# Inverse roots of the last layer norm for groups of four tiles instead of two, their rows scaled two steps later

## The reference

```
x = _layernorm(x + _L0_gnn_ref(x, ...))                 # attention over the edges into a node
x = _layernorm(x + _L1_gnn_ref(x, edge_attr_64, ...))   # attention with edge features and a gated skip
_layernorm(x): (x - mean) / sqrt(var + 1e-5)            # over the 256 features of a row
```

## Time and profile before

| | |
|---|---|
| time, three runs | 1277.13 us median (1275.6 to 1277.79) |
| the profiled execution | 1276.99 us |
| its span, first to last instruction | 1275.2 us |
| mean granted TensorE clock | 0.978 of full speed |
| busy share of the span | PE 92%, DVE 82%, POOL 67%, ACT 65% |
| the stage Output | from about 1092 us to the end |
| chain that ended last, by engine | PE 59%, DVE 15%, issue 12%, POOL 7%, ACT 3% |

### The profile page before, as it was taken

The page is one execution under the profiler, slowest core; times in us unless marked ns, Lnnn a source line. Parts: engine busy times, 40 slices in busy tenths (PEclk is TensorE's granted clock), DMA queues, the critical chain, the costliest instruction groups (busy, mean ns, idle before and its releaser), DMA issues.

```text
span 1275.2 us, 28369 instructions
## 1 busy us (share of the span) xinstructions
PE 1171.5 (92%) x6982; PEld 1022.2 (80%) x6982; DVE 1044.4 (82%) x3794; ACT 830.0 (65%) x2783; POOL 852.2 (67%) x1074
## 2 busy tenths in 40 slices
PE   2899999999998699999999699999999995799995
PEld 2788999989896478888878599899999994688884
DVE  2667777777778789999999799999999987789895
ACT  0366666666667766666666766656666668589996
POOL 6688888888873355545554567677666753288887
PEclk9899999999999899999999999999999998799998
DMA  7568888888884388778887787777767743355652
GB/s 209 164 223 288 268 271 262 260 272 268 267 265 133 100 273 261 246 252 252 259 249 235 214 241 210 217 220 220 224 201 220 226 144 110 124 184 187 185 192 94
DMA packets 208795, 276.99 MB, mean 217 GB/s; under 512 B 40044, under 2 KB 140419, under 8 KB 208633
## 3 DMA queue, kind: packets, MB, share of 16 engines
q1 hardware_dynamic: 187913, 223.83, 55.8%
q0 software_dynamic: 19264, 50.85, 13.2%
q10 hardware_dynamic: 1456, 0.49, 0.2%
HBM read 159.67 MB, written 117.12 MB: 217 GB/s over the span
## 4 chain that ended last, share of the span: by engine, by line
PE 59%; DVE 15%; issue 12%; POOL 7%; ACT 3%; DMA 2%; another core or an unknown queue 1%; SPq 1%; DVEq 0%; POOLq 0%; ACTq 0%
PE banks L751 20%; PE banks L864 7%; PE banks L741 6%; PE banks L1392 5%; POOL out L1545 4%; PE banks L854 3%; PE banks L1227 3%; POOL output_r L1551 3%; DVE AT L1253 3%; PE banks L866 3%; PE banks L1379 2%; PE banks L1397 2%; PE banks L1220 2%; PE banks L953 2%; PE banks L1377 2%
## 5 line engine op out<-in xcount | busy, mean ns | idle before, releaser
L751 PE MATMUL banks<-m_ext,node_XT 128*128 128x257 f32 x1568 | 376.6, 383 | 0.1
L751 PEld LDWEIGHTS banks<-m_ext,node_XT 128*128 128x128 f32 x1568 | 285.7, 192 | 32.9 <-issue 0.3
L777 DVE SCALAR_TENSOR_TENSOR node_X<-banks,node_be,node_X 128x256 f32<-128x256 f32 x392 | 169.5, 474 | 82.1 <-ACT node_be L703 54.2
L678 POOL TENSOR_TENSOR node_r<-node_vv,half 128x4 f32<-128x4 f32 (+1 forms) x202 | 214.0, 1059 | 17.0 <-POOL node_vv L673 0.2
L709 ACT ACTIVATE node_XT<-banks 128x512 f32<-128x512 f32 x196 | 117.3, 599 | 131.0 <-PE banks L741 122.3
L673 POOL TENSOR_SCALAR node_vv<-node_mv 128x4 f32<-128x4 f32 (+1 forms) x202 | 58.2, 288 | 196.9 <-DVE node_mv L785 177.7
L716 ACT ACTIVATE node_sq<-node_X 128x256 f32<-128x256 f32 x392 | 157.8, 408 | 0.0
L690 ACT ACTIVATE node_X<-node_X,node_r 128x256 f32<-128x256 f32 x326 | 146.0, 496 | 1.4 <-POOL node_r L678 1.4
L770 DVE BATCH_NORM_STATS2 node_st<-node_X 128x6 f32<-128x256 f32 x392 | 145.5, 413 | 1.6 <-issue 1.0
L741 PE MATMUL banks<-ident,node_X 128*128 128x128 f32 x784 | 122.5, 280 | 20.1 <-issue 10.8
L831 POOL DMA_INDIRECT ring<-in_x,src_col x100 | 107.0, 1070 | 26.4 <-issue 14.4
(11 more groups left out here) (265 smaller groups left out, 2731.4 us busy)
## 6 DMA issues: line engine op xcount, KB each, us to landing
node_X<-in_x SPq DMA_DIRECT2D x196, 256.0 KB
out<-node_X SPq DMA_DIRECT2D x196, 256.0 KB
ring<-rows SPq DMA_DIRECT2D x210, 128.0 KB
rows<-ring SPq DMA_DIRECT2D x100, 256.0 KB
rows<-ring SPq DMA_DIRECT2D x200, 128.0 KB
MB<-keeps SPq DMA_DIRECT2D x40, 320.0 KB, 4.6
store<-rows SPq DMA_DIRECT2D x90, 128.0 KB
MB<-picks SPq DMA_DIRECT2D x50, 128.0 KB
```

The lines of the kernel that those rows point to most:

```text
L678: pool.tensor_tensor(r[:, s % 4, NT * lo:NT * hi], v, self.c.half[:, NT * lo:NT * hi], ALU.pow).then_inc(self.roots, 1)
L751: last = pe.matmul(ps[:, NT * o + k, 0:D + 1], self.XT[:, o, k * D + h * P:k * D + (h + 1) * P], c.m_ext[:, h, :], start=(h == 0), stop=(h ...
L777: last = dve.scalar_tensor_tensor(out=X[:, n % U, k, :], in0=ps[:, b + k, 0:D], scalar=self.be[:, n % 4, k:k + 1], in1=X[:, n % U, k, :], ...
```

## The change

The groups become two single tiles, 23 groups of four (tiles 2 to 93) and three pairs (tiles 94 to 99). Rows of a group of more than two are scaled from step last+9 on instead of last+7. So every row n of a group of four is scaled in step n+12 (row k has n = last-3+k, and its step is last+9+k) and scattered in step n+13. The pairs at the end keep last+7, but the running maximum holds them back: row 93 is scaled in step 105, and rows 94 to 97 then in step 105 too, 98 in step 106 and 99 in step 107. Scatters 93 to 97 all stand in step 106. The pow and the epsilon stay in step last+6; the tiles `half_row`, `va` and `r` grow from two to four columns by `max(GROUPS)`.

```
-GROUPS = (1, 1) + (2,) * 48 + (1, 1)
+GROUPS = (1, 1) + (4,) * 23 + (2,) * 3
...
-        _at = max(_last + 7 + _k, _at)
+        _at = max(_last + (9 if _size > 2 else 7) + _k, _at)
```

## The result

The changed kernel takes 1302.22 us (median of four runs, 1300.01 to 1303.68), the kernel before 1277.33 beside it: a ratio of 1.0187 (95% interval 1.016 to 1.0214). The forecast was 1279.9 with a range up to 1281.7. The direction was right, the size was not: some 25 us were lost where 2.6 to 2.9 were expected, far outside the range.

What follows compares the result with a forecast made beforehand. PE (3.276 us a pair) and POOL (3.29) were taken as both full, with POOL's remaining scatters setting the end. Scatter 86 comes 4.36 later, the way on is 1.44 shorter: +2.9 on 1276.99 gives 1279.9, range 1277.4 to 1281.7.

Steps and rivals of the forecast that it cites:

- In mid-stage nobody waits for a scatter: Output, mid-stage: scattering row n in step n+13 instead of n+9 costs nothing there, as the rows' places aren't used again.
- L1602 at 1.638 throughout: Sign of a right forecast: the product L1602 starts every 1.638 us a tile through Output, tile 99's about 1.1 us earlier.
- Fewer pows: POOL in Output: four tiles cost 1065 ns of pow instead of 1500; worth at most PE's 1.1 us of stall.
- Two steps later: Scales in Output: ACT's 18.0 us of waiting for pows go, hidden behind PE, worth nothing beyond the 1.1 us.
- The debt at the end: End of Output: POOL works off four steps of scatters alone; scatter 99 starts at 1275.34 instead of 1272.42, +2.9 us.
- first leg: End of Output, L1602 of tile 95 to scatter 86: from 1252.37 to 1255.50, with 0.80 from scale end to scatter.
- That PE has reserve and follows a relieved GpSimd: Rival, Output's mid-stage: the stage runs at POOL's new 1.54 us a tile, 9.6 us go, about 1270; 5 in 100.
- The rival with a smaller debt: Rival, end of Output: the 0.30 of issue before each scatter vanishes, leaving +0.8, 1277.8; 12 in 100.
- the rival with a larger debt: Rival: PE's 1.1 us of stall stays or a POOL stall falls into the last 20 us, 1281 to 1281.4; 15 in 100.
- The prediction's list of signs: Wrong if: PE's spacing under 1.638, POOL late in mid-stage, end scatters closer than 1.28, or last scatter no later than 1272.4.

Runs made afterwards that it cites:

- The delay alone: Pairs as in the kernel before, but their rows scaled two steps later (step last+9): 1280.34 against 1280.53 of the kernel before, ratio 0.9987.

## Why the prediction was wrong

*The step that failed.* The prediction's sentence is "In mid-stage nobody waits for a scatter", and with it "L1602 at 1.638 throughout". TensorE's pace was taken as its own, and with plain transfers it is: nothing that the profile shows holds TensorE up there from 1160 to 1255 us. What was left out is that the time from its matmul to the reader's start depends on what GpSimd issues at that moment. Indirect scatters 1.3 us apart made that time up to 1.6 us longer. Scan, next L1598 and the transposed copy hang on it in a loop of little reserve, and PE lost 1.05 us in each group from tile 18 on: its way became 20.5 us longer, not 1.1 shorter. In Output before, two scatters and a pow were far enough apart, three starts in 3.3 us, so the rows that the prediction used could not show it.

The trace of before does show it, in a stage that the prediction never looked at. In Score GpSimd issues two indirect gathers a tile (L831), often four in a run, and ScalarE waits 38.9 us for L866 and 32.8 for L854 of TensorE between 60 and 380 us. One case, from the timeline of the kernel before:

```profile
157.08 0.95 POOL L831 DMA_INDIRECT ring<-in_x,dst_col  x1 [0.31 <-issue]
...
158.19 0.50 PE L866 MATMUL banks<-w_ad,ST 128*128 128x4 f32 x4
...
158.33 0.95 POOL L831 DMA_INDIRECT ring<-in_x,src_col  x1 [0.30 <-issue]
...
159.16 0.39 ACT L886 ACTIVATE store<-banks 128x260 f32<-128x260 f32 x1 [1.36 <-PE banks L866]
```

L866 ends at 158.69 by the profile, and ScalarE, idle, starts on its result 0.47 later; the gather at 158.33 is the third in 2.66 us (the first started at 155.67). By the records 71 of 283 updates of TensorE are late in that stage (10 to 400 us), none of 342 from 400 to 700, where GpSimd issues no indirect transfer, and 14 of 367 from 700 to 1090, where its gathers (L1317) mostly stand 3.3 us apart. Some of those waits in Score have other reasons too, so the rows alone would not have given a price, but they hold the effect.

*Fewer pows.* Right as to GpSimd: the pow of four is 1.04 (1.065 taken), the waits of ACT for it are gone, and with most of the scatters away PE's way is 159.97, 1.13 less than before, where the prediction had "at most PE's 1.1 us". But the pow that was removed as a cost had kept the scatters apart. That is the use of it that wasn't seen.

*Two steps later.* Right: hidden. The delay alone takes the stall of 1.1 away, and brings no other.

*The debt at the end.* Right in its steps; that the sum fits to 0.05 us is luck. From L1602 of tile 99 to the last scatter the prediction has 1275.34 - (1259.50 - 1.1) = 16.9; measured 16.85. Its first leg fits: from L1602 of tile 95 to scatter 86 it has 1255.50 - 1252.37 = 3.13, and 3.13 it is. Then one more late result of TensorE makes two legs longer, and the two cancel: the way from scatter 86 to scatter 99 takes 21.12 instead of 19.84, since the pow between 86 and 87 waits 1.40 us for its epsilon, and TensorE takes 7.41 from tile 95 to tile 99 instead of 6.07. The end of GpSimd's timeline after, against the earlier trace rows:

```profile
1295.05 0.98 POOL L1545 DMA_INDIRECT out<-store,last_col  x1 [0.30 <-issue]
1296.34 0.98 POOL L1545 DMA_INDIRECT out<-store,last_col  x1 [0.30 <-issue]
```

The spacing is 1.29, against the 1.28 taken. Scatters follow one another there too, seven in a row, and cost nothing more, since TensorE has no work left. Had the middle stayed, 16.85 - 12.92 - 1.1 = 2.8 us is about what the kernel would have lost, as forecast; no run shows that end without the loss in the middle.

*The rivals.* That PE has reserve and follows a relieved GpSimd is out: with plain transfers GpSimd waits for ScalarE in mid-stage, and L1602 still comes every 1.64 us. The Trainium skill (Perfetto Trace Analysis, Identifying the Most-Contended Engine) judges TensorE's headroom by its weight-load busy time, and by its share of peak arithmetic, which no run here gives; by the first a share of 84% would leave room. The starts of L1602 say that there is none. The rival with a smaller debt is out: the 0.30 of issue stands before each of the last scatters. Of the rival with a larger debt the condition did occur, GpSimd's 1.40 us of waiting near the end, but by TensorE's late result and not by GpSimd's own lateness. None of the rivals had a new loss in mid-stage. The prediction's list of signs named a spacing *under* 1.638 as wrong, not one above. The one that was missing is "four indirect transfers in a row make results of TensorE late"; its condition stands in the code, and its sign in the rows of Score.

*What stays open.* That the readers start late is in the rows. Ends of matmuls are modelled, so a matmul's true end isn't on record, but the times of the updates say that the signal is held up, at least in part. The three updates of a step (L1598, L1602, L1584) come 0.44 and 0.22 us apart when they are on time (1209.38, 1209.82 and 1210.04); in the case above they came at 1208.42, 1208.46 and 1208.50. Of the 81 late updates of the changed kernel 29 follow another late one by 0.042 or 0.043 us. Matmuls whose updates otherwise lie 0.2 to 0.4 us apart are not likely to end that close together, which argues that the earlier ones were done before their signal came. Where in the chip an indirect transfer and TensorE's signals meet isn't shown. Nor is it shown what about the indirect transfer does it. It differs from the plain one in three things at once: the row addresses from a table, the scattered places, and GpSimd's time on it, some 1.0 us against 0.55. An indirect transfer to rows in order, and plain transfers issued back to back while TensorE works, were not run.

## What to carry to other kernels

Before an instruction is taken off an engine, look at what it kept apart: here a pow of 0.75 us spaced GpSimd's indirect transfers, and without it another engine's results came late by more than the pow had cost. A change that leaves the sum of an engine's work alone, or lowers it, can still lose by its order, so write the new order of its DMAs out, start by start, and look through the whole trace, other stages too, for a stretch that has that order under load, and at who waits there. And judge an engine's slack between two others by starts (PE's way), not by busy time: all shares fell here while the kernel got slower.

## What was not expected of the hardware

- With indirect scatters of 128 rows, three starts within some 2.6 us, TensorE's results reached VectorE and ScalarE up to 1.6 us late in the changed kernel. With three starts in 2.95 to 3.05 us a late update is on record in 7 of 17 cases, with 3.3 next to none. In the same stretch no recorded update of VectorE, ScalarE or GpSimd was over 12 ns late, so of the engines' updates on record only TensorE's were.
- Late updates of TensorE come in a row, 0.042 to 0.043 us apart, though on time they lie 0.2 to 0.4 us apart, as if they had been held and let go together.
- It isn't the bytes and isn't GpSimd's load as such: plain transfers of 128 rows as close as that left PE's way at 159.97, and so did pows in the place of three of four scatters.
- An instruction of 0.12 us between two scatters didn't help (PE's way 181.92); 0.4 us more of plain idle time did (165.98).
- A plain transfer of 128 rows took GpSimd 0.54 to 0.60 us, an indirect one of the same rows 0.97 to 1.04.
